# Exponentials first in the steps of a cross-attention, and three kinds of copies moved to other steps

## What is computed

```
x = x + window_attention(layernorm(x))          # 16 heads of 32, windows of 64
x = x + cross_attention(layernorm(x), ctx)      # below
x = x + top1_expert_ffn(layernorm(x))           # 8 experts

# cross_attention: ctx is 32 x 375 x 256; 16 heads of 128, 8 key/value heads
q = h @ Wq;  k = ctx @ Wk;  v = ctx @ Wv        # each k, v head serves two q heads
p = softmax(q @ k.T / sqrt(128), masked)        # 112 x 375 per head
out = (p @ v) @ Wo
```

## Time and profile before

| | us |
|---|---|
| median of 3 runs | 2688.05 |
| the profiled execution, its own time | 2685.35 |
| its span, first to last instruction | 2683.7 |
| window attention, ahead of the cross-attention | 0 to about 474 |
| cross-attention | about 474 to 2395 |
| the 256 steps | 511 to 2385 |
| expert feed-forward | from about 2395 |

### The profile page before, as it was taken

How to read it: one execution, slowest core, us unless ns; L and a number is a source line. 1 busy time by engine, 2 the same in 40 slices (tenths; PEclk the granted TensorE clock), 3 DMA queues, 4 the chain that set the end, 5 groups by cost and what they waited for, 6 DMA issues and landing times. The chain is left out here.

```text
span 2683.7 us, 46237 instructions
## 1 busy us (share of the span) xinstructions
PE 2482.7 (93%) x14850; PEld 2257.6 (84%) x14851; DVE 1733.0 (65%) x4899; ACT 1241.2 (46%) x3183; POOL 1030.1 (38%) x1424
## 2 busy tenths in 40 slices
PE   6899897799999999999999999999999999979488
PEld 5888886788989898889989898898989888869376
DVE  7878886565575657566575756656565665644466
ACT  4555553454454545445454545445454454522211
POOL 4334443243343434334353534334343343431422
PEclk9999998899999999999999999999999999975699
DMA  8322332412122112212121211111111111122654
GB/s 256 95 71 84 96 108 89 162 50 66 62 75 66 62 54 74 74 52 83 52 91 58 88 55 53 54 41 55 51 57 54 53 55 41 41 72 70 220 178 129
DMA packets 108892, 217.87 MB, mean 81 GB/s; under 512 B 20336, under 2 KB 48720, under 8 KB 108416
## 3 DMA queue, kind: packets, MB, share of 16 engines
q1 hardware_dynamic: 103440, 188.42, 21.9%
q0 software_dynamic: 5040, 16.58, 1.7%
q10 hardware_dynamic: 224, 10.49, 1.2%
HBM read 134.57 MB, written 91.36 MB: 84 GB/s over the span
## 5 line engine op out<-in xcount | busy, mean ns | idle before, releaser
L1171 POOL TENSOR_SCALAR x_probs<-x_probs,x_inv 112x376 f32<-112x376 f32 x512 | 639.3, 1258 | 273.6 <-DVE x_inv L1323 273.6
L1165 POOL TENSOR_SCALAR x_bias<-x_top 112x1 f32<-112x1 f32 x512 | 129.1, 252 | 871.8 <-DVE x_top L1295 864.9
L1215 ACT ACTIVATE x_probs<-x_probs,x_bias 112x376 f32<-112x376 f32 x512 | 307.0, 603 | 105.2 <-POOL x_bias L1165 104.7
L1380 PE MATMUL x_ps_o<-x_pT,x_v 128*128 128x224 f32 (+1 forms) x2304 | 310.3, 279 | 43.2 <-DVE x_pT L1302 42.5
L1380 PEld LDWEIGHTS x_ps_o<-x_pT,x_v 128*128 128x128 f32 (+1 forms) x2304 | 288.0, 192 | 69.6 <-DVE x_pT L1302 61.5
L1380 PE MATMUL x_ps_f<-x_xT,x_wq 128*128 128x448 f32 x1536 | 339.3, 371 | 4.5 <-issue 4.5
L1380 PE MATMUL x_ps_f<-x_wo,x_oT 128*128 128x512 f32 x1344 | 315.7, 391 | 1.0 <-DVE x_oT L1311 1.0
L1380 PE MATMUL x_ps_s<-x_kT,x_qT 128*112 128x376 f32 x1536 | 314.6, 340 | 1.5 <-DVE x_top L1295 1.5
L1380 PE MATMUL x_ps_f<-x_ctxT,x_wk 128*128 128x376 f32 x1536 | 306.4, 335 | 1.9 <-DVE x_ctxT L1272 1.9
L1380 PEld LDWEIGHTS x_ps_f<-x_xT,x_wq 128*128 128x128 f32 x1536 | 282.4, 189 | 26.5 <-issue 4.7
L1380 PEld LDWEIGHTS x_ps_f<-x_wo,x_oT 128*128 128x128 f32 x1344 | 252.6, 189 | 50.0 <-issue 1.2
(11 more groups left out here) (186 smaller groups left out, 3799.5 us busy)
## 6 DMA issues: line engine op xcount, KB each, us to landing
x_ctxs<-x_ctxT SPq DMA_DIRECT2D x32, 752.0 KB, 3.8
x_ctxT<-x_ctxs SPq DMA_DIRECT2D x32, 752.0 KB, 4.3
x_xT<-h2T SPq DMA_DIRECT2D x16, 896.0 KB, 5.0
m_rows<-slots SPq DMA_DIRECT2D x35, 258.0 KB, 3.0
slots<-w_blank SPq DMA_DIRECT2D x8, 1032.0 KB, 5.2
x_ctxn<-in_ctx_dram SPq DMA_DIRECT2D x32, 256.0 KB
m_hn<-in_L_ffn_W_dram SPq DMA_DIRECT2D x32, 256.0 KB
w_xa<-in_x_dram SPq DMA_DIRECT2D x32, 224.0 KB, 3.3
```

The lines of the kernel that those rows point to most:

```text
L1165: pool.tensor_scalar(bias[:, m:m + 1], top[:, m:m + 1], -0.1 * NEG, -SCALE, ALU.max, ALU.mult) \
L1171: pool.tensor_scalar(probs[0:T, m, 0:SE], probs[0:T, m, 0:SE], inv[:, m:m + 1], None, ALU.mult).then_inc(normed, 1)
L1215: act.activation(probs[0:T, m, 0:SE], probs[0:T, m, 0:SE], ACT.Exp, bias=bias[:, m:m + 1], scale=SCALE, accum_out=total[:, m:m + 1]).then_ ...
L1380: last = pe.matmul(out, w, r, start=m == 0, stop=m == len(jobs) - 1)
```

## The change

Four things, all in `cross_attention`:
- ScalarE's list begins a step with `exps(i)`, ahead of the copies of the early fills; VectorE's has `inverses(i)` right behind `maxima(i)`, ahead of the low parts of the early fills. VectorE's `add` of O stands behind `out(i-2)` instead of ahead of it.
- The context fills C stand in step g = 2 instead of g = 3, for TensorE, ScalarE and VectorE alike. In a step with O, `ORDER` then has K, C, C, O.
- The four input pieces stand in the steps g = 1 and g = 2 of the passes with b % 4 = 1 and 2, instead of all four steps of b % 4 = 1, and at the end of the step on both engines. The weight splits also go to the end of their steps.
- The mask row of pass b+1 is made at the end of step g = 1 of pass b, instead of at the start of step g = 0 of b+1.

```diff
@@ early_fills
-        if g == 3 and b + 2 < B:
+        if g == 2 and b + 2 < B:
             out += [("C", b + 2, 0), ("C", b + 2, 1)]
         if g == 2 and b in TILE_OF:
             out.append(("O", TILE_OF[b], 0))
@@ x_piece
-        return b // QUAD + 1 if b % QUAD == 1 and b // QUAD + 1 < NB // QUAD else None
+        if b // QUAD + 1 == NB // QUAD or b % QUAD not in (1, 2) or g not in (1, 2):
+            return None
+        return b // QUAD + 1, 2 * (b % QUAD - 1) + g - 1
@@ ScalarE
                 for i in range(STEPS):
-                    for p in splits_at(i):
-                        split(p)
+                    exps(i)
                     for f in early_fills(i):
                         if f[0] != "O":
                             fill(f)
-                    exps(i)
-                    if x_piece(i) is not None:
-                        split_x(x_piece(i), i % G)
                     if i >= 2:
                         out(i - 2)
                     for f in before_transposes(i):
@@
                     for f in behind_transposes(i):
                         fill(f)
+                    if x_piece(i) is not None:
+                        split_x(*x_piece(i))
+                    for p in splits_at(i):
+                        split(p)
@@ VectorE
+                mask_row(0)
                 for i in range(STEPS):
-                    if i % G == 0:
-                        mask_row(i // G)
                     maxima(i)
-                    for p in splits_at(i):
-                        split(p)
+                    inverses(i)
                     for f in early_fills(i):
                         if f[0] != "O":
                             fill(f)
-                    inverses(i)
-                    if x_piece(i) is not None:
-                        split_x(x_piece(i), i % G)
+                    if i >= 2:
+                        out(i - 2)
                     for f in early_fills(i):
                         if f[0] == "O":
                             add(f)
-                    if i >= 2:
-                        out(i - 2)
                     for f in before_transposes(i):
                         fill(f)
                     if i >= 1:
                         probsT(i - 1)
                     for f in behind_transposes(i):
                         fill(f)
+                    if i % G == 1 and i // G + 1 < NB:
+                        mask_row(i // G + 1)
+                    if x_piece(i) is not None:
+                        split_x(*x_piece(i))
+                    for p in splits_at(i):
+                        split(p)
```

## The result

The changed kernel takes 2810.4 us, the median of 4 runs (2804.9 to 2814.3), beside 2687.6 us for the kernel before in the same comparison: a ratio of 1.0457, with a 95% interval of 1.0443 to 1.0470. It is **slower by 4.6%**; the forecast was 2815 us, in a range from 2755 to 2855. One execution of all those reported here, of the version with C back in g = 3 in the version from the theory, ran at a mean granted clock of 0.827 and took 2803.9 us; it is left out of that version's time.

What follows compares the result with a forecast made beforehand. The prediction took TensorE, busy 93% of the span, as the bound, with only its waits to win. From the profiled execution, 2685.35 + 69 + 26 + 32 = 2812.4 us, as a median 2815 us, range 2755 to 2855.

Steps and rivals of the forecast that it cites:

- Part 1: Exponentials first: K low part ends 3.2 us behind the start of `maxima`; VectorE's light step becomes 4.24 us, from 3.66.
- Part 2: Context copies in g = 2: O waits for the K copy, 14 times 2.5 us and 11 times 3.1, 69 us.
- the ledger: The prediction's account of VectorE's lateness against TensorE, giving O's waits as 69 us and `pv`'s as 84 us.
- Part 3: Light steps: `pv` waits 84 us for the transposed probabilities instead of 58.0, +26 us, bounded at 0 and +40.
- Part 4: TensorE's clock: the 25 new waits bring 20 falls at 1.6 us each, +32 us, with ends 0 and 40.
- the clock term: The +32 us for falls of TensorE's clock behind O's new waits, 20 falls at 1.6 us.

Runs made afterwards that it cites:

- the version from the theory: Kernel before, with input pieces and the next pass's mask row in steps with O, and C in g = 2 behind O: 2653.5 us, ratio 0.9884.
- the filler run: Changed kernel, with 9 more unused TensorE products in each of the 25 steps with K, C, C, O, while O waits: 2782.4 us, ratio 1.0360.

## Why the prediction was right

Point by point, by its own steps:
- *Part 1.* The last reciprocal ends 2.59 us behind `maxima` in practically every step, and the K low part 3.15 us behind it; forecast 2.60 and 3.2. VectorE's light step is 4.20 or 4.26 us in most of the steps in which it is late, forecast 4.24.
- *Part 2.* O waited 68.4 us on its weight loads in the 25 steps, forecast 69; in step 66 it started 5.17 us into the step, forecast 5.2. In the 14 passes without an input piece the wait was 2.4 to 2.5 us with one of 3.0, in the 11 with one it was 2.9 with one of 4.1 (forecast 2.5 and 3.1); the two long ones are in passes with weight splits, which the ledger didn't have here, and they make up for 2.9 in place of 3.1. The run with O ahead of C shows that the bank is the cause. The forecast that O would wait 0.6 even with the old order held too (0.74 in the run of C in g = 2 alone).
- *Part 3.* The forecast was 84 us, 26 more than before; `pv` waits 88.0, which is 26.5 more than the 61.5 of before. The forecast's 58.0 and 84 both lack the two waits behind the last steps; without them it is 84.6. The ledger's terms hold one by one as well: forecast 21, 42, 19 and 2 us, measured 21.1, 41.0, 18.6 and 3.9. The `add` of O is worth 21.8 of them, which the run with the add ahead shows.
- *Part 4.* This term was the right mechanism and too large: 32 us forecast, about 20 measured. The price of a fall was right (1.6 us, by the filler run); their number was 14 of 25, not 20, and the kernel before had one itself, which the forecast didn't take off. By the Trainium skill's table (TensorE: Matmul & The Clock Gate, "Why this matters for your kernels") this term would have been nearly nothing; the filler run shows 1.6 us for each fall.
- *What was not on the list:* waits of other fills for the K copy, 4.7 us; the scores, whose weight loads sat idle 4.9 us instead of 1.8 for no cause that the profile names.

The terms as measured are 68.4 and 4.7 less the 3.0 of small waits that only the kernel before had, 26.5, 3.1, and 21.9 less the 1.6 of the one earlier fall. They come to 120.0 us, against the 120.3 by which the steps grew; another 2.4 us lie outside of the steps, where nothing was changed. The forecast's 127 us came close to the span's 122.7 in part by luck: the clock term was 12 too high, and the things that weren't on the list, 7 us in all, point the other way.

The ledger was weaker away from the changed kernel. It took VectorE's lateness to be paid only at `pv`. Where C's copies stand behind the exponentials in a light step, the next K fill waits for the context that they make (32.3 us with C back in g = 3, 15.7 with exponentials first alone, where 54 us were measured and 31 forecast). And its light step of 3.66 us holds only while GpSimd isn't in the way: in the version from the theory the second light step in a row took 4.0 us, and 3.67 once the bias had left GpSimd. Behind the change VectorE's step of 4.2 us covers that, so it didn't count.

Is the change as a whole a bad idea? Its parts are not alike: mask rows and input pieces gain 25 us alone, exponentials first costs 54 alone, the `add` costs some 22 in waits inside the change, and the context copies cost 22 alone and some 83 inside the change (1.0457 less 1.0149 with C back in g = 3, of 2686), because the K copy that O waits for had just been made later: O waits 19.3 us with C moved alone, 26.7 with all but exponentials first, 68.4 with both. Two of the parts lengthen the same wait, and the clock adds to it.

## What to carry to other kernels

Where fills rotate through a few banks, a fill that is inserted changes which copy the later ones wait for: write down, for each fill, whose copy frees its bank, and when that copy ends in the other engine's list; do the same for the data that it reads, since a wait on a fill can be for either. Moving a copy behind a latency chain that it used to cover costs its whole length at each step in which that engine is late, and a small instruction (here the `add`) is free only as long as it stands ahead of a wait. Work without a due time belongs where its engine already waits for a long product, in front of that wait rather than at a step's end (2650.4 against 2659.1 us here).

## What was not expected of the hardware

Pauses of about the same length do and don't bring a fall of TensorE's clock. In the changed kernel 25 pauses of TensorE of 2.2 to 3.8 us gave 14 falls to half, and seven that all lasted 2.2 us gave four; in the steps of the kernel before there was one fall. A fall costs 1.6 us here, which is more than half of the wait that brought it. Added work that no one uses made the kernel 26 us faster, 22 of them in the steps; the other 4 us are nearly all behind the last step, where the two kernels are alike. The stretch took 309.1 us at a mean clock of 0.73 in the changed kernel and 305.4 at 0.75 with the filler; over all the kernels here it lies between 302.6 and 309.6 us, so this part isn't shown to be a gain of the filler's.
